# The routing weights of a linear-attention block on eight cores: two steps fused on the Vector engine, two steps on GpSimd dropped

## What is computed

```python
xn  = layernorm(x)                                   # per token, 1024 features
# linear attention, 8 heads of 64, decay gamma = sigmoid(decay_log)
q = elu(xn @ W_Q.T) + 1;  k = elu(xn @ W_K.T) + 1;  v = xn @ W_V.T
# per token t: S = gamma*S + k_t v_t^T;  z = gamma*z + k_t
#              out_t = (q_t S) / (q_t . z + 1e-6)
attn = (out * sigmoid(xn @ W_g.T + b_g)) @ W_O.T
# feed-forward: one linear layer plus a routed low-rank term, 8 experts, rank 4, top 2
scores  = softmax(xn @ gate_w.T)                     # 8 per token
weights, idx = top_k(scores, 2)
lora = sum over the two experts of weights * (xn @ left[idx]) @ right[idx]
result = x + attn + (xn @ W_lin.T + b_lin) + lora
```

## Time and profile before

| | us |
|---|---|
| median of 3 runs | 449.46 (448.91 to 450.83) |
| the profiled execution | 450.61 |
| span of its slowest core (core 5) | 449.5 |
| spans of the eight cores | 443.4 to 449.5 |

### The profile page before, as it was taken

How to read it: one execution, slowest core, us unless ns; L and a number is a source line. 1 busy time by engine, 2 the same in 40 slices (tenths; PEclk the granted TensorE clock), 3 DMA queues, 4 the chain that set the end, 5 groups by cost and what they waited for, 6 DMA issues and landing times.

```text
span 449.5 us, 6528 instructions; the slowest of 8 cores (443.4 to 449.5 us)
## 1 busy us (share of the span) xinstructions
PE 316.6 (70%) x2066; PEld 143.4 (32%) x2066; DVE 205.2 (46%) x807; ACT 131.3 (29%) x281; POOL 32.2 (7%) x96
## 2 busy tenths in 40 slices
PE   0004975218989988368889893489899884799866
PEld 0002332103344433223444342234444332334421
DVE  5031544023555437343656264635555466254641
ACT  3754221654033233325313244130112331300000
POOL 8200002100000000220000000300000003000000
PEclk9999988556999999559999997679999996689977
DMA  7999992000211220000221100001101100010111
GB/s 176 168 260 192 163 161 40 1 0 1 95 40 55 96 93 1 1 1 1 93 95 50 47 1 0 1 1 48 47 2 48 47 2 1 0 48 2 47 48 47
DMA packets 12851, 24.96 MB, mean 56 GB/s; under 512 B 2929, under 2 KB 7153, under 8 KB 12818
## 3 DMA queue, kind: packets, MB, share of 16 engines
q0 software_dynamic: 7856, 7.49, 12.0%
q1 hardware_dynamic: 4962, 17.05, 10.7%
HBM read 23.63 MB, written 8.39 MB: 71 GB/s over the span
## 4 chain that ended last, share of the span: by engine, by line
PE 56%; ACT 13%; DVE 13%; issue 9%; POOL 4%; DMA 1%; DVEq 1%; ACTq 0%; SPq 0%; POOLq 0%
PE pQK L791 14%; PE pG L587 7%; PE pQK L803 7%; PE pA L396 5%; PE pQK L396 5%; PE pO L583 4%; PE pV L583 4%; ACT scr1b L285 3%; PE pQK L795 2%; DVE S_sb L721 2%; PE pT L339 2%; ACT gsig L595 2%; PE pQK L798 2%; DVE A_sb L632 1%; ACT scr1b L288 1%
## 5 line engine op out<-in xcount | busy, mean ns | idle before, releaser
L791 PE MATMUL pQK<-wlin_sb,xnfm 128*128 128x512 bf16 x256 | 66.4, 406 | 0.2
L812 DVE TENSOR_TENSOR out_sb<-pQK,x_sb 128x512 f32<-128x512 f32 x32 | 22.1, 691 | 76.7 <-PE pQK L803 76.7
L587 PE MATMUL pG<-wg_sb,xnfm 128*128 128x512 bf16 x128 | 55.0, 429 | 0.0
L583 PE MATMUL pO<-wv_sb,xnfm 128*128 128x512 bf16 x64 | 30.0, 468 | 19.9 <-DVE den_r L733 19.2
L595 ACT ACTIVATE gsig<-pG 128x512 bf16<-128x512 f32 x16 | 9.6, 598 | 110.0 <-PE pG L592 99.2
L791 PEld LDWEIGHTS pQK<-wlin_sb,xnfm 128*128 128x128 bf16 x256 | 24.8, 103 | 29.3 <-issue 7.7
L803 PE MATMUL pQK<-wo_sb,ygfm 128*128 128x512 bf16 x128 | 34.0, 389 | 0.0
L583 PE MATMUL pV<-wv_sb,xnfm 128*128 128x512 bf16 x64 | 25.2, 395 | 9.7 <-DVE den_r L733 6.7
L411 ACT ACTIVATE phir<-phiw 128x512 bf16<-128x512 f32 x32 | 19.9, 630 | 35.1 <-DVE phiw L405 35.0
L632 DVE TENSOR_TENSOR A_sb<-pA,masks 128x128 bf16<-128x128 f32 x64 | 18.1, 282 | 21.3 <-PE pG L619 21.3
L754 DVE SCALAR_TENSOR_TENSOR ygtm<-gsig,den_r,pA 128x64 bf16<-128x64 bf16 x128 | 26.0, 275 | 0.5
(11 more groups left out here) (139 smaller groups left out, 488.7 us busy)
## 6 DMA issues: line engine op xcount, KB each, us to landing
x_sb<-x SPq DMA_DIRECT2D x16, 512.0 KB, 8.2
out<-out_sb SPq DMA_DIRECT2D x16, 512.0 KB, 2.8
wlin_sb<-wlin POOLq DMA_DIRECT2D x1, 2048.0 KB, 60.3
wq_sb<-wq POOLq DMA_DIRECT2D x1, 1024.0 KB, 24.4
wk_sb<-wk POOLq DMA_DIRECT2D x1, 1024.0 KB, 37.5
wv_sb<-wv POOLq DMA_DIRECT2D x1, 1024.0 KB, 43.0
wg_sb<-wg POOLq DMA_DIRECT2D x1, 1024.0 KB, 49.1
wo_sb<-wo POOLq DMA_DIRECT2D x1, 1024.0 KB, 61.4
```

Source lines behind the costliest of these rows:

```text
L583: ins = TE.matmul(pVb[:, :], xnfm[:, 1024 * k + cs * 128 : 1024 * k + cs * 128 + 128], wv_sb[:, FH * k : FH * k + FH], start=(k == 0), sto ...
L587: TE.matmul(pG[:, :], xnfm[:, 1024 * k + cs * 128 : 1024 * k + cs * 128 + 128], wg_sb[:, FH * k : FH * k + FH], start=(k == 0), stop=False)
L791: TE.matmul(pQK[bank][:, :], xnfm[:, 1024 * k + cs * 128 : 1024 * k + cs * 128 + 128], wlin_sb[:, D * k + 512 * n : D * k + 512 * n + 512] ...
L812: ins = VE.tensor_tensor(out_sb[:, cp * D + 512 * n : cp * D + 512 * n + 512], pQK[bank][:, :], x_sb[:, cx * D + 512 * n : cx * D + 512 * ...
```

## The change

Three edits in `C_top2`. `tmp2` is made in one step on the Vector engine (`ind1 * -1e30 + e8`, with the constant in the instruction) where there was `i1inv` on the Vector engine and a product on GpSimd; the largest value is pushed far below the others and not set to zero, and the second largest comes out the same. `wt_tm` is made in one step on the Vector engine (`indf * rs8 * e8`, `rs8` one value for each partition) where there was `wtu` on the Vector engine and a product on GpSimd. The waits follow: the Vector engine waits on its own semaphore for `tmp2` and for `rs8`, ScalarE waits for the Vector engine and no longer for GpSimd, and the first wait of `C_top2` also covers the last copy L528 of the block before, since the Vector engine now overwrites `wt_tm`.

```diff
-        VE.wait_ge(s_sca.h, rec["e8b"])
+        VE.wait_ge(s_sca.h, max(rec["e8b"], rec["s_w4"]))
...
         VE.wait_ge(s_gp.h, g_i1)
         for ci in range(4):
             c4 = (blo + ci) % 4
-            ins = VE.tensor_scalar(i1inv[...], ind1[...], -1.0, 1.0, ALU.mult, ALU.add)
-        v_inv = s_vec.inc(ins)
-        GP.wait_ge(s_vec.h, v_inv)
-        for ci in range(4):
-            ins = GP.tensor_tensor(tmp2[...], esl(c4), i1inv[...], ALU.mult)
-        g_t2 = s_gp.inc(ins)
-        VE.wait_ge(s_gp.h, g_t2)
+            ins = VE.scalar_tensor_tensor(tmp2[...], ind1[...], -1e30, esl(c4),
+                                          ALU.mult, ALU.add)
+        v_t2 = s_vec.inc(ins)
+        VE.wait_ge(s_vec.h, v_t2)
...
         VE.wait_ge(s_gp.h, g_ind)
+        VE.wait_ge(s_vec.h, v_rs)
         for ci in range(4):
             c4 = (blo + ci) % 4
-            ins = VE.tensor_tensor(wtu[...], esl(c4), indf[...], ALU.mult)
-        v_wtu = s_vec.inc(ins)
-        GP.wait_ge(s_vec.h, max(v_wtu, v_rs))
-        for ci in range(4):
-            ins = GP.tensor_scalar(wt_tm[...], wtu[...], rs8[:, c4 : c4 + 1], None, ALU.mult)
-        g_wt = s_gp.inc(ins)
-        SE.wait_ge(s_gp.h, g_wt)
+            ins = VE.scalar_tensor_tensor(wt_tm[...], indf[...], rs8[:, c4 : c4 + 1],
+                                          esl(c4), ALU.mult, ALU.mult)
+        v_wt = s_vec.inc(ins)
+        SE.wait_ge(s_vec.h, v_wt)
```

More of the change, by code:

```diff
@@ L489, in C_top2 @@
             c4 = (blo + ci) % 4
-            ins = VE.tensor_scalar(i1inv[:, c4 * E : c4 * E + E],
-                                   ind1[:, c4 * E : c4 * E + E],
-                                   -1.0, 1.0, ALU.mult, ALU.add)
-        v_inv = s_vec.inc(ins)
-        GP.wait_ge(s_vec.h, v_inv)
-        for ci in range(4):
-            c4 = (blo + ci) % 4
-            ins = GP.tensor_tensor(tmp2[:, c4 * E : c4 * E + E], esl(c4),
-                                   i1inv[:, c4 * E : c4 * E + E], ALU.mult)
-        g_t2 = s_gp.inc(ins)
-        VE.wait_ge(s_gp.h, g_t2)
+            ins = VE.scalar_tensor_tensor(tmp2[:, c4 * E : c4 * E + E],
+                                          ind1[:, c4 * E : c4 * E + E],
+                                          -1e30, esl(c4), ALU.mult, ALU.add)
+        v_t2 = s_vec.inc(ins)
+        VE.wait_ge(s_vec.h, v_t2)
         for ci in range(4):
@@ L511, in C_top2 @@
         VE.wait_ge(s_gp.h, g_ind)
+        VE.wait_ge(s_vec.h, v_rs)
         for ci in range(4):
             c4 = (blo + ci) % 4
-            ins = VE.tensor_tensor(wtu[:, c4 * E : c4 * E + E], esl(c4),
-                                   indf[:, c4 * E : c4 * E + E], ALU.mult)
-        v_wtu = s_vec.inc(ins)
-        GP.wait_ge(s_vec.h, max(v_wtu, v_rs))
-        for ci in range(4):
[L519 to L522, removed]
-        g_wt = s_gp.inc(ins)
-        SE.wait_ge(s_gp.h, g_wt)
+            ins = VE.scalar_tensor_tensor(wt_tm[:, c4 * E : c4 * E + E],
+                                          indf[:, c4 * E : c4 * E + E],
+                                          rs8[:, c4 : c4 + 1], esl(c4),
+                                          ALU.mult, ALU.mult)
+        v_wt = s_vec.inc(ins)
+        SE.wait_ge(s_vec.h, v_wt)
         for ci in range(4):
```

## The result

The changed kernel takes 438.41 us (median of 8 runs, 437.42 to 439.30) against 449.91 for the kernel before on the same chip (8 runs): a ratio of 0.9741, 95% interval 0.9722 to 0.9760, 11.5 us less. The forecast was 443.8 with a range from 439.5 to 447.0: right in its direction, and too small by half. Some executions of a kernel are in a slower state, in which the cores of a die show a lower clock and the time is some per cent longer; ratios and means here are of the others.

A forecast was written before the change was run, and what follows sets the result against it. The prediction took the routing weights' chain of waits ahead of `E_vg` as the bound: 1.90 us a block, 7.6 in four, less 1.9 for the clock, is 5.7 off 449.46, so 443.8 us, range 439.5 to 447.0.

The forecast's parts named there:

- What bounds the kernel: Once per block, the small routing steps of `C_top2`, copies and transposition hold up `E_vg` while TensorE idles: 19.4 us waited.
- tmp2: Fusing this step in `C_top2` on the Vector engine gains 0.84 us a block, between 0.6 and 0.9.
- wt_tm: Fusing this step in `C_top2` on the Vector engine gains 1.06 us a block, between 0.8 and 1.25.
- The added waits: New waits in `C_top2`: 0.09 us on the Vector engine's own semaphore, 0.05 for `rs8`, nothing for the first wait.
- what is late next: Ahead of `E_vg`: the reciprocal of the denominators does not take over, so `E_vg` starts the whole 1.9 us earlier.
- What the clock takes back: TensorE's clock rise in `E_vg` stays in two blocks and moves in two: 1.9 us of the gain given back.
- rival 5: `E_vg` and the first half of `G_out` run slow in every block: slower, 455 us; chance 0.02.
- rival 2: TensorE's clock stays up over the shortened gap ahead of `E_vg`: 439.7 us for one block, 435.3 for three; chance 0.10.
- The inner range of the forecast: Range of the likeliest case for the whole kernel: chain gain 5.6 to 8.6 us, clock 0.95 or 2.85 us.
- 1 (the rise follows, 441.9): TensorE's clock rise follows the start of `E_vg` in every block, so the whole 7.6 us stays: 441.9 us; chance 0.17.
- 3: TensorE's clock rise in `E_vg` stays at its moment in every block: 3.8 us gained, 445.7 us; chance 0.15.
- 4: In the routing chain, slow fused instructions or another wait let little through: within 0.5% of before, 448 us; chance 0.06.

The follow-up runs named there:

- e1: Only `tmp2` fused, `wtu` and GpSimd's `wt_tm` product kept, against the kernel before: ratio 0.9928.
- e2: Only `wt_tm` fused, `i1inv` and GpSimd's `tmp2` product kept, against the kernel before: ratio 0.9825.
- e4: Changed kernel plus matmuls nobody reads ahead of `E_vg` (4 per block, 14 in the first): 435.77 us, 0.9686 of the kernel before.
- e10: Changed kernel with all routing on the Vector engine and four copies of 32 values instead of 16 copies: 428.92 us, 0.9476 of the kernel before.
- e11: Changed kernel with table loads moved into ScalarE's idle time, all routing on the Vector engine and four copies: 416.52 us, 0.9210 of the kernel before.
- e7: Changed kernel plus 17 unread ScalarE copies of 8 values per block, delaying the transposition 1.79 us: 448.0 us.
- e12: Changed kernel plus 19 unread ScalarE copies of 8 values per block: 448.5 us, where the kernel before took 451.3.
- e13: Changed kernel plus GpSimd products beside the chain that nobody waits for, four behind `ind1` and four behind `indf`: 441.08 us, 0.9769 of the kernel before.
- e5: Changed kernel plus 8 unread ScalarE copies of 8 values per block, delaying the transposition 0.84 us: 442 us, given for it and its pair partner.
- e6: Changed kernel plus 10 unread ScalarE copies of 8 values per block, delaying the transposition 1.05 us: 445.1 us.
- e9: Changed kernel plus one-column activations where ScalarE is idle, moving eight table loads earlier: 430.06 us, 0.9521 of the kernel before.
- e8: Changed kernel plus 35 unread ScalarE copies of 8 values per block, delaying the transposition 3.68 us: 451.7 us.

## Why the prediction was wrong in its size

**What bounds the kernel** was right: the routing weights stood on the chain once per block, with nothing beside them, in the first block as well as in the others.

**`tmp2`.** Right: 0.41 us for the group where 0.40 was taken, 0.10 for the wait on its own semaphore (185.01 to 185.11) where 0.09 was, 0.82 us won a block (e1) where 0.84 was forecast.

**`wt_tm`.** Right in kind, a little low in price: 0.65 us for the four with a per-partition value, where 0.60 was taken from the rows of the state update; 0.98 us won a block (e2) where 1.06 was forecast. Together 7.3 us and not 7.6.

**The added waits** cost nothing that shows, apart from 0.07 for `rs8` where 0.05 was priced, and **what is late next** was right: the reciprocal did not take over, and `E_vg` moved with the copies. TensorE's waits at the transposition fell from 19.4 to 14.0 us, not to 12, since L539 was shorter in three of the four blocks (11.3 us together on core 1 after, 13.4 on core 5 before) and so left more to wait.

**What the clock takes back** is the step that failed: 1.9 us given back were forecast, and on the mean core 2.7 us came on top (1.6 in `E_vg`, 1.1 in L791), on the slowest core 3.5. Two errors are in it. The first is the assumption that the rise stays in two blocks of four; the distances went from 6.0, 3.9, 4.4 and 5.7 us to 4.0, 2.7, 5.7 and 3.4, so in three of four it came sooner after the start, and only in the third later. In the mean of the eight cores `E_vg` got shorter in every block, by 0.5, 0.5, 0.6 and 0.1 us. The second weighs more: I treated the clock's part as a line (half of each microsecond), and it is a stair. Both slow L791 of the slowest core followed the longest slow stretches, 6.0 and 5.7 us, and either of these blocks had next to nothing left to lose by a shift. The sum had no term for them; they stood in rival 5 as something that may get worse, and in rival 2 as a side remark. The slowest of eight cores is the one that has drawn such blocks, and a shift draws again. By the rows of before alone the sign should have been open, with a range from about 4 given back to 4 on top; the stated lower end of 439.5 missed by 1.1 us for that reason. The inner range of the forecast, 441.5 to 446, doesn't follow from its own terms either: they give 449.46 - 8.6 + 0.95 = 441.8 to 449.46 - 5.6 + 2.85 = 446.7.

The rule of the Trainium skill that I weighed, "TensorE: Matmul & The Clock Gate", section "What's actually happening" (what watches the activity is not reset by the kernel's start), is neither contradicted nor tested by any run here: shifts of 0.12 us a block moving the time by microseconds are what one would see if rises come at moments that the work doesn't set. But with a rise that stays in all four blocks it would give 3.8 us, and 11.5 were measured. As I read it, the rule tells that the position matters, not which way a given shift goes.

The rivals: 1 (the rise follows, 441.9) was nearest and still too high. 2 (the clock holds over the gap) did not happen in the changed kernel, where every `E_vg` still has a slow stretch (on cores 0 and 6 the clock was still up at its start in the fourth block and fell within the first matmul); it happened in e4, and at the start of 19 of e10's 32 `E_vg` and 15 of e11's. 3, 4 and 5 were wrong. The 1.1 us ahead of the first `ind1` on the slowest core had no term either and can't be predicted from one trace.

Open is what is left of e7 and e12: the profiles place it in the fourth block's clock, one profiled execution each, and one or two microseconds of a cost of GpSimd's own can't be excluded by e13, though the pairs e5/e2 and e6/e1 speak against it. Open is also the 0.9 us of the result outside the chain, `E_vg` and L791. That the whole result returns when the transposition goes back was shown only for three quarters of it (8.4 of 11.7 us).

## What to carry to other kernels

A chain of tiny steps that changes engine at each one is paid in full where a queue stands behind it, and its price can be worked out from durations and handoffs to a tenth of a microsecond: 1.90 predicted, 1.83 measured. Where TensorE restarts behind such a wait, add a term for its clock with both signs, count the slow stretches and what is slow behind them on every core, and expect a stair; two shifts that differ by 0.1 to 0.2 us a block can differ by 4 us in the time. To compare two versions of such a kernel, compare the mean of the cores and the parts of it, beside the slowest core. Once a chain of waits is on the path, look at every link of it: table loads, the steps left on GpSimd and small copies on the same chain gave as much again as the change itself (0.9210 against 0.9741, 416.5 us). But a link that the profile puts on the chain need not give its length when it goes: the exponential loads gave 0.46 us of 1.28. And a total that agrees with the forecast is no proof of its terms (e9).

## What the runs showed of the hardware that was not expected

The fused instruction on 128 x 8 values costs 160 ns with a constant and 221 ns with a per-partition value; in a group of four they follow each other by 0.08 and by 0.14 us. A kernel's time is not smooth in a delay: 0.12 to 0.2 us a block more (7.14 and 7.06 to 7.26) cost 4 us, and 1.6 us a block more than before (e8) cost 2.4 us where the chain is 6.5. A faster `E_vg` can make the work behind it slow: with the clock up from its first matmul (3.55 us), its counterpart to L791 was slow behind 13 of 32 in e4, while behind the 30 of the changed kernel that were partly slow but under 6 us long it was slow behind none. In both, 2.5 us with little work on TensorE lie between `E_vg` and L791. With 1.2 to 1.4 us there, as in e9 and e11, L791 was fast behind all 64, whatever `E_vg` did: taking the sigmoid's table load off that wait, 1.28 us, also removed the slow L791, 1.4 us each. A table load in front of a chain of exponentials gave only 0.46 us of its 1.28 when it was moved away.
